# GpSimd takes every residual addition from the second batch on

## The reference, cut to what matters

```
h = layernorm(x) * (1 + ca) + sa
x = x + ga * gelu(h @ (w2 @ w1 * sparse_mask).T + b2)     # the "attention" stage
h = layernorm(x) * (1 + cb) + sb
x = x + gb * ffn(h)        # low-rank: U1 (1024x256), V1, silu(gate)*up, U2, V2
```

## Time and profile before

| what | value |
|---|---|
| median of 3 runs | 1194.72 us (1193.59 to 1196.96) |
| the profiled execution | 1194.4 us, its span 1192.6 us |
| busy over the span | PE 96%, DVE 49%, ACT 41%, POOL 33% |
| chain that ended last | PE 83%, DMA 6%, DVE 4%, ACT 3%, POOL 1% |
| GELUs (L1002) | x64, from 94.6 to 268.3 us |
| gate products on GpSimd (L1557) | x64, 85.2 us |
| additions on GpSimd (L1560) | x46, 60.5 us |
| additions on the vector engine (L1235) | x18, 0.669 to 1.498 us each, median 1.117 us |

### The profile page before, as it was taken

How to read it: one execution, slowest core, us unless ns; L and a number is a source line. 1 busy time by engine, 2 the same in 40 slices (tenths; PEclk the granted TensorE clock), 3 DMA queues, 4 the chain that set the end, 5 groups by cost and what they waited for, 6 DMA issues and landing times.

```text
span 1192.6 us, 15379 instructions
## 1 busy us (share of the span) xinstructions
PE 1144.0 (96%) x5882; PEld 942.7 (79%) x5882; DVE 585.7 (49%) x938; ACT 491.6 (41%) x787; POOL 391.9 (33%) x339
## 2 busy tenths in 40 slices
PE   5588999998999999999999999999999999999998
PEld 5357898897777788888888888888888888888886
DVE  1557687786665334534434344443443444444343
ACT  0037577676778543224223323322422331332241
POOL 1007899891112667323031130312303113031210
PEclk9799999999999999999999999999999999999999
DMA  9984998857553642421040150122104015013101
GB/s 360 357 311 152 333 350 300 306 191 279 212 210 124 198 137 93 160 88 71 20 157 1 71 176 1 71 88 89 71 30 148 2 69 177 1 71 96 47 1 70
DMA packets 57485, 169.61 MB, mean 142 GB/s; under 512 B 6208, under 2 KB 11072, under 8 KB 55360
## 3 DMA queue, kind: packets, MB, share of 16 engines
q1 hardware_dynamic: 57408, 168.57, 39.3%
HBM read 126.51 MB, written 42.04 MB: 141 GB/s over the span
## 4 chain that ended last, share of the span: by engine, by line
PE 83%; DMA 6%; DVE 4%; ACT 3%; issue 2%; SPq 1%; POOL 1%; DVEq 0%; ACTq 0%
PE bank L543 21%; PE bank L544 21%; PE bank L545 21%; PE bank L708 6%; PE bank L603 3%; PE bank L905 2%; PE bank L912 2%; PE bank L907 2%; DMA mask_b<-in_mask 2%; PE bank L582 2%; ACT nrm L976 2%; PE bank L694 1%; DVE h_lo L1340 1%; DMA pt_dram<-pt_st 1%; DVE bn L1207 1%
## 5 line engine op out<-in xcount | busy, mean ns | idle before, releaser
L1140 ACT ACTIVATE act<-bank,b_sb 128x512 f32<-128x512 f32 (+1 forms) x176 | 121.3, 690 | 497.2 <-PE bank L545 481.4
L1472 DVE SCALAR_TENSOR_TENSOR act<-bank,b_sb,act 128x512 f32<-128x512 f32 (+1 forms) x176 | 131.9, 750 | 377.8 <-PE bank L545 354.3
L543 PE MATMUL bank<-pt,v_hi 128*128 128x512 f32 x688 | 268.7, 391 | 1.3 <-DVE act L1472 1.3
L544 PE MATMUL bank<-pt,v_hi 128*128 128x512 f32 x688 | 267.7, 389 | 0.0
L545 PE MATMUL bank<-pt,v_lo 128*128 128x512 f32 x688 | 267.7, 389 | 0.0
L1629 POOL TENSOR_TENSOR x2t<-gbb_bc,x2t 128x512 f32<-128x512 f32 x64 | 86.8, 1379 | 247.5 <-DMA x2t<-x_dram 247.5
L1482 DVE TENSOR_TENSOR act_lo<-act,act_hi 128x512 fp32r<-128x512 f32 (+1 forms) x176 | 159.0, 903 | 0.9
L543 PEld LDWEIGHTS bank<-pt,v_hi 128*128 128x128 f32 x688 | 129.1, 188 | 31.6 <-DVE act L1472 4.3
L545 PEld LDWEIGHTS bank<-pt,v_lo 128*128 128x128 f32 x688 | 129.1, 188 | 26.8
L544 PEld LDWEIGHTS bank<-pt,v_hi 128*128 128x128 f32 x688 | 129.2, 188 | 26.4
L543 PE MATMUL bank<-act_hi,u_hi 128*128 128x512 f32 x336 | 131.0, 390 | 0.8 <-DVE act_lo L1482 0.7
(11 more groups left out here) (135 smaller groups left out, 1660.9 us busy)
## 6 DMA issues: line engine op xcount, KB each, us to landing
wm_sb<-in_wmod SPq DMA_DIRECT2D x9, 2048.0 KB, 10.4
xs<-in_x SPq DMA_DIRECT2D x32, 512.0 KB, 5.3
x_dram<-xs SPq DMA_DIRECT2D x32, 512.0 KB, 4.8
xs<-x_dram SPq DMA_DIRECT2D x32, 512.0 KB, 5.6
x2t<-x_dram SPq DMA_DIRECT2D x32, 512.0 KB, 4.0
out<-x2t SPq DMA_DIRECT2D x31, 512.0 KB, 4.9
pt_dram<-pt_st SPq DMA_DIRECT2D x8, 1024.0 KB, 7.4
pt<-pt_dram SPq DMA_DIRECT2D x8, 1024.0 KB, 5.7
```

The lines of the kernel that those rows point to most:

```text
L543: nc.tensor.matmul(acc, s_hi, m_hi, start=start, stop=False)
L544: nc.tensor.matmul(acc, s_hi, m_lo, start=False, stop=False)
L1140: nc.scalar.activation(act[0:w, j % 2, :], bank[0:w, j % 2, :], ACT.Silu, bias=b1_sb[0:w, i, 0:1]).then_inc(silu_done, 1)
L1472: nc.vector.scalar_tensor_tensor(act[0:w, j % 2, :], up, b1_sb[0:w, i, 1:2], act[0:w, j % 2, :], ALU.add, ALU.mult).then_inc(act_done, 1)
```

## The change

`on_vector` is now true only for the odd units of batch 0. Those were already the vector engine's units in batch 0 (1, 3, 5 and 7), so batch 0 is the same program as before. In batches 1 to 7 the units 3 and 7 go from the vector engine to GpSimd: 14 additions of 128x512. Each of them now follows its gate product in GpSimd's queue, and the three places where the vector engine did them are gone.

```diff
         def on_vector(b, u):
-            return u % TT == TT - 1 or b == 0 and u % TT == 1
+            return b == 0 and u % 2 == 1
...
                 lo(b, 4)
                 lo(b, 5)
-                if b > 1:
-                    add(b - 1, 7)
                 lo(b, 6)
...
                 lo(b + 1, 1)
-                add(b, 3)
                 stats(t, 2)
...
                 if b == 0:
                     beta2_rows()
-                    add(NB - 1, 7)
                 else:
                     pt_lo(b - 1)
```

## The result

The changed kernel takes 1197.12 us (median of 20 runs, 1195.32 to 1199.74) against 1195.12 us for the kernel before on the same chip (20 runs, 1193.14 to 1197.75). The ratio is 1.0019, with a 95% interval from 1.0011 to 1.0026: slower by 2 us, 0.2%. The profiled execution has a span of 1195.1 us against 1192.6.

The account below looks back on a forecast made before the run. TensorE bounds the middle batches, vector-engine additions batches 1, 5 and 6; after the change GpSimd's cycle limits. The 3.1 us saved are lost waiting; 1194.4 + 1.1 = 1195.5 us, read as 1195.6; 8-in-10 range 1192.5 to 1199.2.

Parts of the forecast that it names:

- the likeliest case: Whole kernel: time within 0.3% of the kernel before, chance 0.76.
- GpSimd's cycle: GpSimd, per attention batch: eight product-and-addition pairs and one shift block take 22.64 us, against TensorE's 21.89.
- The second rival: GpSimd in the attention batches: operations stay stretched, cycle 23.5 us, total about 1199.8 us; chance 0.17.
- Shift 8 at 251.1: GpSimd, end of five cycles from batch 2 on: the shift for ScalarE's next norm is there at 251.1 us.
- turn(8, 0) 0.5 to 0.7 us late: TensorE in batch 7: turn(8, 0) comes 0.5 to 0.7 us later than before, behind the late norm.
- The last addition at 273.65: GpSimd at the attention stage's end: add(7, 7) ends at 273.65 us, against 272.54 on the vector engine before.
- The gain of the vector engine: TensorE in batches 1, 5 and 6: fewer vector-engine additions save 1.2 + 0.97 + 0.96 = 3.1 us.
- the forecast's list of signs: Trace signs of being right, among them batches 5 and 6 without TensorE's wait for lo.
- the standstill: TensorE in batch 7, near 253 to 256 us: a wait for nrm, about 3 us (2 to 3 among the signs).
- The third rival: TensorE's clock after batch 7's wait: some 4 us at half speed cost 2 us, total about 1197.5; chance 0.05.
- The forecast's 1.1 us: Attention stage's exit: later last addition delays the store, the reload of x and the chain behind by 1.1 us.

Follow-up runs that it names:

- unit 3 back: Against the changed kernel, unit 3 is back on the vector engine, unit 7 stays on GpSimd: 1195.86 us, ratio 0.9998 to the kernel before.
- shift ahead of unit 7: The changed kernel with GpSimd's rstd_and_shift(b + 2) moved ahead of unit 7: 1200.32 us, ratio 1.0045 to the kernel before.
- the swap: TensorE's two If blocks reordered, untaken one first: changed kernel 1199.30 us, kernel before 1198.30, version with only unit 3 moved 1195.34.

## Why the prediction was right or wrong

The measured 1197.1 us lies in the range, and the change is a loss of under 0.3% as the likeliest case had it. The loss is about twice the forecast's size (2.0 us in the medians, 2.5 in the spans, against 1.1). The forecast took 0.3% for the least that can be told from no change; with 20 executions each, 0.2% could be. The mechanism was right as far as GpSimd goes: its lag costs, first at turn(8, 0) and then at the last addition. That the total came out in the range owes something to luck, since two terms of 0.3 to 1.6 us on TensorE were not in the sum. Step by step:

- **GpSimd's cycle: right.** Forecast 22.64 us, measured 22.62 in batch 3, with the operation that was L1540 at 0.21 us. The second rival (stretches that stay) is out.
- **Shift 8 at 251.1: right** (251.37). turn(8, 0) 0.5 to 0.7 us late: measured 0.85. TensorE waits 2.16 us there, forecast "about 3": it is the 1.3 us that TensorE had gained by then and the 0.85 that it comes late.
- **The last addition at 273.65: right within 0.3** (273.91).
- **The gain of the vector engine: too large.** I took 1.2 + 0.97 + 0.96 = 3.1 us for batches 1, 5 and 6. From the first GELU of a batch to that of the next those batches are 23.64, 22.66 and 22.43 us against 24.36, 22.85 and 22.85, so 0.72 + 0.19 + 0.42 = 1.3 us. The run with only unit 3 moved got 0.74 + 1.10 + 0.96 = 2.8. So batch 1 gives 0.7 us in either kernel, and the 1.2 was too much by itself. In batches 5 and 6 the changed kernel still waits for lo (0.65 and 0.26 us), which the forecast's list of signs had ruled out. This did not reach the total, because GpSimd was the limit anyway; it made the standstill shorter than forecast. A part of the reason is on the vector engine. The last operation of the gate clamp in batch 5, before and then after:

```profile
217.56 0.19 DVE L1280 SCALAR_TENSOR_TENSOR gate_feat<-gate_sign,gate_big 128x32 f32<-128x32 f32 x1
```

```profile
216.71 1.21 DVE L1280 SCALAR_TENSOR_TENSOR gate_feat<-gate_sign,gate_big 128x32 f32<-128x32 f32 x1
```

  It takes 1.21 instead of 0.19 us. Before, it fell into the 0.23 us in which GpSimd waited for a GELU (217.49 to 217.72). In the changed kernel a gate product runs on GpSimd from 216.60 to 217.88, and the operation ends with it. It is a matter of how the two engines meet, and not of GpSimd's idle time alone: with only unit 3 moved, that idle time is filled too, and there the operation starts in the 0.08 us between two of GpSimd's operations and takes 0.19 us. The Trainium skill (SBUF — State Buffer, Who interferes with whom) has the rule: a vector instruction with two SBUF inputs, as this one, contends with a GpSimd instruction that reads SBUF, and the one that issues second blocks until the first is through. The trace agrees, with 1.02 us more behind a product of 1.28. So the two engines do meet elsewhere than at semaphores. The prediction cited the rule but counted nothing for it on the vector engine's side.
- **The clock: I gave it 0.05, and it came.** The third rival had the price (2 us) near: 1.6 us in one execution, behind the standstill that it named, and 0.9 us in the other, behind the exit, where it had not looked. "1.00 throughout, an idle stretch of 1.24 us included" was no evidence for a stretch of 2.2 us. But it is not shown that the clock makes 2 us out of 1: in the first execution the reload alone would have held TensorE to within 0.2 us of where it was.
- **The exit gap: not in the sum at all.** It was 1.24 us before and 2.42 and 1.57 us in the two executions of the changed kernel. It is 1.1 to 1.2 us in two other kernels (unit 3 back; shift ahead of unit 7) and 2.4 to 2.6 in five. The kernels with the short gap show the instruction queue's packet 1 to 2 us ahead of TensorE's last product of the stage, those with the long one show it at or behind it (before: at 266.5 to 267.0 us, with the start of the last product at 267.8; changed kernel: at 269.0 to 269.5, with it at 268.7). What sets that moment stays open; the swap shows only that the gap belongs to the jump.

How late TensorE is against the kernel before, in us, in the two executions of the changed kernel:

| what | first | second |
|---|---|---|
| turn(8, 0), behind the standstill | 0.85 | 0.89 |
| longer exit gap | 1.18 | 0.33 |
| what is left up to turn(9, 0): the clock | 0.92 | 1.64 |
| turn(9, 0) | 2.95 | 2.86 |
| statistics on the reloaded x | 2.77 | 0.61 |
| turn(9, 3) | 2.77 | 2.51 |
| span | 2.5 | 2.4 |

The forecast's 1.1 us was the path over the last addition and the reload. That path was there: the last addition came 1.37 us later, and shift 9 and the reload hold TensorE wherever it is early, as the swap and the early shift show. What the forecast left out is what can come on top of it. In the second execution TensorE's own path is later, by the exit gap and the clock. In the first the reload took 1.4 us longer than before, and why it takes 6.2 to 8.6 us in one and the same kernel stays open. Which of these makes up the 0.9 us between the forecast and the medians is not shown.

## What to carry to other kernels

Before a queue is given the work of another engine, add up its cycle against the pace of the bottleneck in that stage, not over the span: here 22.6 against 21.9 us, with an idle share that looked like 67% over the span. Then ask where the lag first has no slack. Work given back helps only where the queue does not wait for its input anyway. Where two paths end close together, here TensorE's own and the reload, a gain on one of them is worth only the distance to the other. And when a forecast has TensorE stand still for 2 us or more at a place where it had been dense, the clock behind it belongs in the sum, as a chance. Of four executions with a standstill of 2.2 us in batch 7 one lost the clock behind it, for 1.6 us. All six with an exit gap of 2.4 us or more lost it there, for 0.9 us each, and none of the four with a gap of 1.1 to 1.6 us did.

## What the hardware showed that I had not expected

Leaving an If block on TensorE by a jump over an untaken block shows as a wait for "issue" of 1.1 to 2.6 us at the stage's exit; with the untaken block first, the wait is 3.1 to 5.0 us at its start. Two executions of one kernel lost TensorE's clock at different places, 14 us apart, and took the same time, one held by the reload and one by TensorE. And the vector engine, 76% busy in batch 5 (17.24 of 22.58 us), has an operation that lengthens sixfold (0.19 to 1.21 us) without any change to it, when it issues behind a GpSimd operation and not between two.
